# End of attention in a fused attention and mixture-of-experts kernel: three moves in the written order of the work

## The reference

```
q, k, v = x @ Wq + bq, x @ Wk + bk, x @ Wv + bv
attn    = softmax(where(causal, q @ k.T / sqrt(64), -inf))
x       = layernorm(x + concat_heads(attn @ v) @ Wo + bo)
xn      = layernorm(x) * gamma + beta
probs   = softmax(xn @ router_w.T / 1.5);  w, idx = top_k(probs, 2)
y       = sum over the 2 chosen experts of w * (silu(xn @ W1[e]) @ W2[e])
out     = layernorm(y + x)
```

## Time and profile before

| | |
|---|---|
| median of three runs | 1298.41 us |
| profiled execution: time, span | 1298.3 us, 1296.6 us |
| TensorE matmul busy | 1273.5 us (98%) |
| ScalarE busy | 1158.6 us (89%) |
| VectorE busy | 1094.0 us (84%) |
| GpSimd busy | 748.4 us (58%) |
| mean granted TensorE clock | 0.996 |

### The profile page before, as it was taken

The page is one execution under the profiler, slowest core; times in us unless marked ns, Lnnn a source line. Parts: engine busy times, 40 slices in busy tenths (PEclk is TensorE's granted clock), DMA queues, the critical chain, the costliest instruction groups (busy, mean ns, idle before and its releaser), DMA issues.

```text
span 1296.6 us, 36408 instructions
## 1 busy us (share of the span) xinstructions
PE 1273.5 (98%) x11106; PEld 1129.2 (87%) x11106; DVE 1094.0 (84%) x5167; ACT 1158.6 (89%) x3655; POOL 748.4 (58%) x1333
## 2 busy tenths in 40 slices
PE   7999999999999999999999999999998999999997
PEld 6888888888888888888888888888887999999993
DVE  6888888888888888888888888888897798788857
ACT  7999999999989998899899999899886999999957
POOL 2346666666555655556656655555556676555545
PEclk9999999999999999999999999999998999999999
DMA  5000000000000000000000000000032232222229
GB/s 210 6 14 22 23 22 23 23 24 28 19 14 15 14 14 14 14 14 14 14 14 14 15 14 16 16 21 17 14 144 91 69 89 84 76 78 78 69 82 339
DMA packets 49215, 60.98 MB, mean 47 GB/s; under 512 B 8304, under 2 KB 35059, under 8 KB 48768
## 3 DMA queue, kind: packets, MB, share of 16 engines
q1 hardware_dynamic: 39376, 41.44, 9.9%
q0 software_dynamic: 8640, 17.13, 3.9%
q10 hardware_dynamic: 1008, 0.08, 0.1%
HBM read 30.72 MB, written 28.81 MB: 46 GB/s over the span
## 4 chain that ended last, share of the span: by engine, by line
PE 91%; ACT 4%; DVE 1%; issue 1%; DMA 1%; POOL 0%; ACTq 0%; SPq 0%; POOLq 0%; DVEq 0%
PE ps_a L1261 15%; PE ps_s L1304 13%; PE ps_s L1283 11%; PE ps_b L1296 7%; PE ps_f L1339 7%; PE ps_s L1261 7%; PE ps_f L1296 6%; PE ps_b L1555 4%; PE ps_s L1286 4%; PE ps_a L1555 4%; PE ps_b L1261 4%; PE ps_f L1261 3%; PE ps_s L1620 2%; PE ps_a L1360 1%; ACT f_y L682 1%
## 5 line engine op out<-in xcount | busy, mean ns | idle before, releaser
L682 ACT ACTIVATE f_y<-f_y,neg_max 128x256 f32<-128x256 f32 x512 | 256.5, 501 | 45.6 <-DVE neg_max L962 45.6
L962 DVE CUSTOM_DVE_ANT_0 f_y<-ps_s,mask 128x256 f32<-128x256 f32 x512 | 214.6, 419 | 62.3 <-PE ps_s L1286 62.0
L1261 PE MATMUL ps_a<-xt_hi,weights 128*128 128x256 f32 x1024 | 241.5, 299 | 0.0
L581 POOL TENSOR_TENSOR ot_lo<-f_y,ot_hi 128x512 fp32r<-128x512 f32 x128 | 164.9, 1288 | 115.9 <-PE ps_s L1286 110.6
L978 DVE TENSOR_SCALAR f_y<-f_y,inv_sums 128x256 f32<-128x256 f32 x512 | 194.6, 380 | 7.0
L685 ACT ACTIVATE f_y<-f_y,neg_max 128x128 f32<-128x128 f32 x512 | 200.0, 391 | 0.0
L1304 PE MATMUL ps_s<-ident,f_y 128*128 128x128 f32 x1536 | 196.6, 275 | 0.0
L647 POOL DMA_INDIRECT y_tok<-f_y,m_dest x142 | 140.2, 987 | 88.7 <-DVE m_dest L1167 61.1
L1261 PEld LDWEIGHTS ps_a<-xt_hi,weights 128*128 128x128 f32 x1024 | 175.5, 189 | 16.0 <-issue 10.8
L1283 PE MATMUL ps_s<-qk 64*128 64x256 f32 x1024 | 176.5, 421 | 5.1 <-ACT pt L730 2.3
L1304 PEld LDWEIGHTS ps_s<-ident,f_y 128*128 128x128 f32 x1536 | 172.9, 142 | 5.1 <-issue 0.5
(11 more groups left out here) (227 smaller groups left out, 3467.6 us busy)
## 6 DMA issues: line engine op xcount, KB each, us to landing
m_x<-queue SPq DMA_DIRECT2D x71, 133.0 KB, 2.3
f_y<-y_tok SPq DMA_DIRECT2D x32, 256.0 KB, 6.4
queue<-empty SPq DMA_DIRECT2D x8, 532.0 KB, 3.6
x_raw<-in_x SPq DMA_DIRECT2D x32, 128.0 KB
out_x<-f_y SPq DMA_DIRECT2D x16, 256.0 KB, 6.7
y_tok<-f_y,m_dest POOLq DMA_INDIRECT x142
f_y<-in_w SPq DMA_DIRECT2D x1, 2048.0 KB, 10.9
m_w<-in_w SPq DMA_DIRECT2D x1, 2048.0 KB, 14.8
```

The costliest lines, as they stand in the source:

```text
L581: pool.tensor_tensor(ot_lo[:, first:first + 2, :], ot[:, s % 2], ot_hi[:, first:first + 2, :].bitcast(F32), ALU.subtract).then_inc(ot_lo_d ...
L682: act.activation(row[:, 0:2 * P], row[:, 0:2 * P], ACT.Exp, scale=-1.0, bias=neg_max[:, pair, h, 0:1], accum_out=sums[:, d % 2, pair, h, 0:1])
L962: dve.tensor_tensor_reduce(out=row[:, 0:2 * P], in0=ps_s[:, pair, h, 0:2 * P], in1=mask[:].rearrange("p a b -> p (a b)"), scale=-1.0, scal ...
L1261: ins = pe.matmul(dst, lhs, rhs, start=(i == 0), stop=(i == len(terms) - 1))
```

## The change

- SyncE waits for the first table and the sent tokens, and loads the rows of expert step 0, ahead of the four DMAs of the first weights; `load_rows(1)` stays behind them.
- GpSimd runs `slots(31)` and `send_tokens(31, 0)` right after `norm(31)`. Then it waits until the last probabilities are scaled, and then rounds and splits the outputs of 124 to 127.
- ScalarE runs the two tanh of expert step 0 ahead of `copy_outputs(127)`, then `affine(1)`, and `expert_weights(1)` and `router_exponentials(32)` behind it.
- TensorE transposes the rows of step 0 ahead of z of sequence 31, runs the whole of `hidden(0)` ahead of `outputs(127)`, and takes 6 of the 8 chunks of the last output projection in expert step 0 and 2 in step 1.

```diff
@@ SyncE
+            sp.wait_ge(first_table_done, 1)
+            for par in range(2):
+                sp.wait_ge(tokens_sent[par], (COUNTED + 1 - par) // 2 * TILES * TOP * 16)
+            load_rows(0)
             for par in range(2):
                 sp.wait_ge(w1_stored[par], E // 2 * 16)
             sp.wait_ge(v_ready, SEQS * 4)
             for part in range(4):
                 cols = slice(part * E * HID // 4, (part + 1) * E * HID // 4)
                 sp.dma_start(weights[:, W1_HI:W1_LO].bitcast(F32)[:, cols], w1_rounded[:, cols]).then_inc(w1_hi_loaded, 16)
-            sp.wait_ge(first_table_done, 1)
-            for par in range(2):
-                sp.wait_ge(tokens_sent[par], (COUNTED + 1 - par) // 2 * TILES * TOP * 16)
-            load_rows(0)
             load_rows(1)
@@ GpSimd
             sequences(step)
-            for s in range(LAST - 4, LAST - 2):
-                round_outputs(s)
-                rest_of_outputs(s)
             slots(SEQS - 1)
             send_tokens(SEQS - 1, 0)
-            for s in range(LAST - 2, LAST):
+            pool.wait_ge(probs_done, LAST * 2)
+            for s in range(LAST - 4, LAST):
                 round_outputs(s)
                 rest_of_outputs(s)
             residual_input(SEQS)
@@ ScalarE
             copy_outputs(LAST - 2)
             first_pt(LAST)
             expert_weights(0)
-            copy_outputs(LAST - 1)
-            expert_weights(1)
-            router_exponentials(SEQS)
             for j in range(NJ):
...
                 if j == 0:
+                    copy_outputs(LAST - 1)
                     affine(1)
+                    expert_weights(1)
+                    router_exponentials(SEQS)
@@ TensorE, last step of attention
                     if n == SEQS - 1:
+                        transpose_x(0)
                         pe.wait_ge(z_done, n)
...
                         ins.then_inc(zt_ready, 1)
-                        transpose_x(0)
@@ TensorE, behind attention
             pe.wait_ge(pt_first_done, LAST)
-            hidden(0, range(0, 2))
+            hidden(0)
             pe.wait_ge(ot_done, LAST - 1)
             outputs(LAST - 1)
-            hidden(0, range(2, CH))
...
-                    output_projection(SEQS, range(0, 4))
+                    output_projection(SEQS, range(0, 6))
                 if j == 1:
-                    output_projection(SEQS, range(4, PAIRS))
+                    output_projection(SEQS, range(6, PAIRS))
```

## The result

The changed kernel takes 1301.08 us, the median of 16 runs (1299.90 to 1302.55); the kernel before takes 1298.67 us in 16 runs (1297.82 to 1301.28). The ratio is 1.0017, with a 95% interval of 1.0010 to 1.0024: 2.2 us slower (the medians stand 2.4 us apart), a little less than the 2.6 us that the prediction counted as no change. The forecast was 1299.9. All medians and ratios here are of fast executions; one run of b1 in the slow state, 1764.85 us at a granted clock of 0.66, is left out.

The account below looks back on a forecast made before the run. TensorE bounds the kernel, holding 91% of the chain of waits. The 2.2 us saved at the rows goes back to GpSimd's wait; + 1.5 us at the last projection's copy on 1298.3 profiled gives 1299.8, forecast 1299.9; range 1297.9 to 1302.0.

Parts of the forecast that it names:

- the call of no change: Whole kernel: the time stays within 0.2%, 2.6 us, of the kernel before; chance 0.69.
- one term of the sum: TensorE's `outputs(127)` up to its reader at half clock, ahead of `copy_outputs(127)`: 1.9 us.
- SyncE: Step 0's rows issued at about 981.1, ahead of the reload; the 2.20 us wait of TensorE for them goes.
- its cover: Reload of the weights, 1.6 us late, is in by 991.2, before ScalarE copies them: hidden, cost 0.
- VectorE: Scaling of the last probabilities ends 2 us sooner, at 988, with GpSimd's rounding moved away; no gain by itself.
- GpSimd and ScalarE's wait: `copy_outputs(126)` waits for `rest_of_outputs(124)` behind slots and sends, until 992.9; `hidden(0)` starts 1.3 us late, at 995.7.
- rival (a): GpSimd's sends are slowed by the reload filling the DMA engines, as an earlier pair was: slower, 1301.5; chance 0.20.
- The clock: TensorE's 5.7 us gap brings half clock for `hidden(0)`, 2.9 us, and `outputs(127)`, 1.9: `copy_outputs(127)` at 1000.5 instead of 997.91.
- 0.3 was taken off: At the last projection's copy 1.5 us was taken, not 1.8, since added durations run past the start of what follows.
- Rival (b): TensorE's clock holds, or comes back within `hidden(0)`: 1.6 us off the sum, no change, 1298.3; chance 0.10.
- ScalarE's list: From `copy_outputs(127)` to the last projection's copy: 8.3 us instead of 9.12, two tanh now running ahead.
- All behind moves along: Both ways out of the stretch hang on the last projection's copy; everything behind moves by the same + 1.5 us.

Follow-up runs that it names:

- b1: e3 with SyncE issuing a quarter of the weights' reload, step 0's rows, the other quarters, then later rows once the reload landed: 1297.51 us, ratio 0.9989.
- e1: Changed kernel with GpSimd's list as before (outputs 124 and 125 rounded ahead of slots and sends, no wait for scaled probabilities): 1296.34 us, ratio 0.9981.
- e3: Changed kernel with GpSimd rounding 124 alone ahead of slots and sends, 125 to 127 behind, without the wait for scaled probabilities: 1296.35 us, ratio 0.9980.
- e4: Changed kernel with 22 unread identity matmuls filling TensorE's gap ahead of `hidden(0)`: 1299.91 us, ratio 1.0008.
- e6: Changed kernel with SyncE's list as it was before: 1299.88 us, ratio 1.0009.
- e5: Kernel before with only SyncE's new order, rows of step 0 ahead of the weights' reload: 1297.54 us, ratio 0.9998.
- c2: Changed kernel with 124 rounded first, reload first on SyncE's queue, step 0's rows issued from ScalarE's queue, three filling matmuls: 1299.08 us, ratio 1.0002.

## Why the prediction was right

The measured time lies in the range, 1.2 us above the forecast, and the call of no change came out with 0.4 us to spare. The mechanism was right in its steps; one term of the sum was too small. In brackets is what the prediction had.

**SyncE, right, with its condition.** The rows were issued at 981.39 (981.1) and the reload began at 981.93 (981.5); the rows landed by 983.7 (983 to 984), and TensorE transposed them at 985.74 without a wait. The reload cost nothing here. The prediction gave its cover as 991.2 against 994; e1 and e3 show what it costs with GpSimd's delay gone, 0.9 to 1.0 us, most of it the register load behind the wait.

**VectorE, right.** With GpSimd's rounding moved, the scaling ended at 988.1 (988). In e1, with the rounding beside it, it ended at 989.95 again. That these 2 us are worth anything in time no run shows: in e1 and e3 the reload was the next wait.

**GpSimd and ScalarE's wait, right.** The rest of 124 at 993.46 less the stretch's 0.38 is 993.1 (992.9); the copy of 126 had 5.36 us of idle time. e1 and e3 show this wait to be the loss: without it the same kernel is 4.7 us faster. The rival (a) fell for its reason: the sends stand 1.39 us apart with a DMA share of 1.01 to 1.04 beside them. What held the pair of the earlier trace rows was not full DMA engines alone.

**The clock, right; the half-clock size of one term, wrong.** Half clock came, for both `hidden(0)` and `outputs(127)`. `hidden(0)` took 2.83 us (2.9). `outputs(127)` to its reader took 1001.69 - 998.82 = 2.9 us where the sum had 1.9. I had taken the row of 1.94 us at 995.92 for a half-clock one, though the clock was coming back in it, at 0.59 from 996 to 997. This term is the forecast's miss of 1 us. The sum itself came to + 1.8 at the projection's copy, and 0.3 was taken off for durations that run past the start of what follows. With the term at 2.9 it is + 2.8, and 2.30 was measured: the start of `hidden(0)`, its length and ScalarE's list each ran up to 0.3 us shorter than summed, so taking something off was sound. Another 0.26 us came behind the copy, which makes the 2.56 of the distance. Rival (b), the clock holds, with its 1298.3 us, is what e4 and e6 show in their profiles: - 0.24 and + 0.02 (their medians, 1299.91 and 1299.88, lie higher).

**ScalarE's list, right within 0.3 us**: 1001.69 to 1009.71 is 8.0 us (8.3). TensorE waited 1.18 us for the copy (cover of 1.2), so the split of the projection cost nothing.

**All behind moves along, right here.** From the copy of the projection to TensorE's tail it is 245.08 us before, 245.34 after, 245.06 in e1 and e4. It is no rule: in e5 it is 246.48, since there TensorE, at half clock, and not the copy, set the end of the stretch.

Where the gain of the change went: the 2.2 us of the rows' wait were real, and e1 shows a gain of 0.2% in the time; GpSimd's place for one buffer took it back, and the idle TensorE lost its clock on top, 2.5 us in the profiles of the changed kernel and e4 (1.2 us in their medians).

## What to carry to other kernels

Before a step is moved later in one engine's list, look up who counts on its semaphore, two uses of the buffer further on: here a 1.9 us step behind 4.9 us of other work cost more than all the rest of the change saved. Price a gap of TensorE twice, once for its length and once for the work behind it at half clock, as a loss that some executions have and others not, and read half-clock durations only from rows whose whole length has a granted clock of 0.50. A transfer that is hidden by a delay becomes the next wait once the delay is mended, and with it what stands behind the wait in the same list, here a register load.

## What was not expected of the hardware

The clock did not follow the length of the gaps. It fell behind gaps of 0.79 and 1.00 us in e1, and held over two of 3 us in e6. Runs of one kernel differ in it: e6's runs have 0.999 to 0.994 in the mean and 1298.3 to 1302.8 us, and its slower half is the half with the lower clock. A kernel with a gap there should be judged by many runs.

A small load that was issued behind a large one waited for it, on the same queue or on another: 133 KB of rows beside 2 MB of reload landed 6.0 us after its issue behind the reload, and 7.4 us from ScalarE's queue (c2), against 2.3 us in the changed kernel, where it was issued first.
